# Half the up projections of an attention block, with the swapped rows made by ScalarE, and larger rings of buffers in its experts

## The reference

```python
mod = (_silu(L0_c) @ L0_wmod).reshape(L0_c.shape[0], 6, 1, -1)
sa, ca, ga, sb, cb, gb = (mod[:, 0], mod[:, 1], mod[:, 2], mod[:, 3], mod[:, 4], mod[:, 5])
...
h = _layernorm(x, axis=-1) * (1 + ca) + sa
x = x + ga * _L0_attn_ref(h, ...)
h = _layernorm(x, axis=-1) * (1 + cb) + sb
x = x + gb * _L0_ffn_ref(h, ...)
...
# attention
h = (x - mu) * jax.lax.rsqrt(var + LN_EPS) * ln_scale + ln_bias
c_q = h @ w_down_q.T
c_kv = h @ w_down_kv.T
q = (c_q @ w_up_q.T).reshape(b, s, H, DH).transpose(0, 2, 1, 3)
k = (c_kv @ w_up_k.T).reshape(b, s, H, DH).transpose(0, 2, 1, 3)
v = (c_kv @ w_up_v.T).reshape(b, s, H, DH).transpose(0, 2, 1, 3)
# rotation
rot = jnp.stack([e * cos - o * sin, e * sin + o * cos], axis=-1).reshape(xr.shape)
...
scores = jnp.einsum('bhqd,bhkd->bhqk', q, k) * scale
attn = jax.nn.softmax(scores, axis=-1)
# experts
h = jax.nn.relu(xf * wi @ w1[i] + b1[i])
y = h @ w2[i] + b2[i]
out = jnp.where(wi > 0, y, out)
```

## Time and profile before

| | |
|---|---|
| median of 3 runs | 841.57 us (839.31 to 844.46) |
| profiled execution | 843.6 us, span of its instructions 841.7 us |
| busy: TensorE, VectorE, ScalarE, GpSimd | 806.4, 618.2, 394.2, 652.0 us |
| the same as shares of the span | 96%, 73%, 47%, 77% |
| granted TensorE clock, mean | 0.984 of 2.4 GHz; 0.83 between 790 and 810 us, 1.00 from 60 to 750 us |
| attention | from about 66 to 760 us |
| experts | from there to the end |

### The profile page before, as it was taken

One profiled execution on the slowest core, in us unless ns is written; L12 is line 12 of the kernel. 1 busy time (PEld: TensorE's weight loads), 2 busy tenths in 40 slices (PEclk: granted clock), 3 DMA queues, 4 the chain that ended last, 5 costly groups with the idle time before them and its releaser, 6 DMA issues.

```text
span 841.7 us, 15143 instructions
## 1 busy us (share of the span) xinstructions
PE 806.4 (96%) x5218; PEld 481.3 (57%) x5218; DVE 618.2 (73%) x1204; ACT 394.2 (47%) x636; POOL 652.0 (77%) x341
## 2 busy tenths in 40 slices
PE   4878999999999999999999999999999999999986
PEld 2535556555555555555555555555565555448886
DVE  8887777787778787878777877778777756346644
ACT  3655444444444444444444445544444444435543
POOL 3479998999999797979797989888888787041654
PEclk8979999999999999999999999999999999999989
DMA  9600010101001010101010101010101010452763
GB/s 246 144 1 14 14 27 14 28 14 25 15 13 28 2 39 2 38 3 39 1 39 2 39 1 40 1 27 15 28 1 27 1 27 1 127 181 80 243 217 97
DMA packets 83257, 40.00 MB, mean 48 GB/s; under 512 B 57433, under 2 KB 71136, under 8 KB 83120
## 3 DMA queue, kind: packets, MB, share of 16 engines
q1 hardware_dynamic: 81456, 35.86, 17.9%
q0 software_dynamic: 1728, 3.19, 1.0%
HBM read 31.46 MB, written 8.21 MB: 47 GB/s over the span
## 4 chain that ended last, share of the span: by engine, by line
PE 93%; DVE 3%; DMA 1%; issue 1%; POOL 1%; ACT 0%; POOLq 0%; SPq 0%; DVEq 0%
PE ps_o L488 28%; PE ps_m L451 9%; PE ps_x L439 9%; PE ps_s L472 7%; PE ps_s L474 7%; PE ps_s L478 7%; PE ps_s L476 7%; PE ps_s L539 4%; PE ps_s L677 3%; PE ps_s L497 2%; DVE mx L1219 1%; PE ps_m L506 1%; PE ps_s L687 1%; PE ps_x L687 1%; PE ps_o L687 1%
## 5 line engine op out<-in xcount | busy, mean ns | idle before, releaser
L1040 POOL TENSOR_TENSOR big<-big,probs 128x1024 f32<-128x1024 f32 x180 | 440.3, 2446 | 70.0 <-ACT probs L784 49.9
L1219 DVE TENSOR_REDUCE mx<-ps_m 128x2 f32<-128x1024 f32 x240 | 294.0, 1225 | 108.5 <-PE ps_m L451 108.2
L784 ACT ACTIVATE probs<-ps_s 128x1024 f32<-128x1024 f32 x256 | 248.9, 1024 | 169.1 <-PE ps_s L478 169.0
L488 PE MATMUL ps_o<-probs,c_all 128*64 128x512 f32 x1024 | 247.9, 605 | 0.0
L488 PEld LDWEIGHTS ps_o<-probs,c_all 128*64 128x64 f32 x1024 | 62.1, 136 | 97.2 <-ACT probs L784 41.4
L451 PE MATMUL ps_m<-k_hi,q_hi 64*128 64x512 f32 x480 | 108.4, 444 | 2.2 <-DVE mx L1219 2.2
L472 PE MATMUL ps_s<-q_hi,k_hi 64*128 64x512 f32 x512 | 101.8, 393 | 0.0
L478 PE MATMUL ps_s<-neg_row,one_row 64*128 64x512 f32 x512 | 101.4, 388 | 0.0
L474 PE MATMUL ps_s<-q_hi,k_lo 64*128 64x512 f32 x512 | 101.2, 390 | 0.0
L476 PE MATMUL ps_s<-q_lo,k_hi 64*128 64x512 f32 x512 | 101.2, 389 | 0.0
L451 PEld LDWEIGHTS ps_m<-k_hi,q_hi 64*128 64x128 f32 x480 | 46.6, 183 | 87.3 <-issue 77.0
(11 more groups left out here) (310 smaller groups left out, 997.3 us busy)
## 6 DMA issues: line engine op xcount, KB each, us to landing
big<-in_experts SPq DMA_DIRECT2D x30, 322.0 KB, 3.6
big<-rd_dram SPq DMA_DIRECT2D x60, 128.0 KB, 2.9
big<-in_wqk SPq DMA_DIRECT2D x16, 256.0 KB, 2.7
neg_row<-nm SPq DMA_DIRECT2D x256, 0.5 KB, 2.0
xs_row<-xs_dram SPq DMA_DIRECT2D x6, 390.0 KB, 4.2
big<-in_expert_w SPq DMA_DIRECT2D x8, 256.0 KB, 4.0
xs_dram<-zero SPq DMA_DIRECT2D x2, 990.0 KB, 10.4
xs_dram<-zero SPq DMA_DIRECT2D x2, 960.0 KB, 11.7
```

Source lines behind the costliest of these rows:

```text
L488: ins = nc.tensor.matmul(ps_o[64 * h:64 * h + 64, :], c_all[:, (p // HP) * TB + kt, :], probs[:, st % 4, h, :], start=(kt == 0), stop=(kt ...
L784: nc.scalar.activation(probs[:, st % 4, :, :], ps_s[:, 2 * (st % 2):2 * (st % 2) + 2, :], ACT.Exp, scale=SCALE).then_inc(s["probs"], 1)
L1040: V.tensor_tensor(acc[:, buf(p, half), :, :], first, probs[:, st % 4, :, :], ALU.add).then_inc(s["added"], 1)
L1219: V.reduce_max(mx[:, :, kh, qt], max_banks(q, n), AX.X).then_inc(s["max_reduced"], 1)
```

## The change

In pairs 2 to 15 the twin is left out: a unit is 512 columns of q or k, straight only, two products, made in groups 1, 3, 5 and 7. ScalarE makes the exchanged rows: it copies four blocks of 32 rows from `ps_x` to the SBUF buffer `tmp`, each to the place of its neighbour, after the group's exponentials. VectorE's `turn` is divided into `turn_cos`, `turn_sin` and `turn_sum` and done in the following even group around the second `reduce_max`; `turn_sin` now has both operands and its result in SBUF. ScalarE's `upper` and VectorE's `lower` follow in the next odd group. GpSimd's split has half the columns from pair 2 on. In the experts ScalarE copies the slots of both batches; output buffers are 16 and places for expert weights 10 (the added ones lie in `probs`, free after the attention); SP loads a group's slots ahead of its expert weights, but for batch 1's first group, where the weights come first and the first tile of slots is loaded by itself.

```diff
-NY = 8
+NY = 16
+NI = 10
...
         def unit_banks(q, u):
-            return U_BANKS[u] if q < 2 else (ps_x[:, 0:QUART], ps_x[:, QUART:HALF])
+            return U_BANKS[u] if q < 2 else (ps_x[:], tmp)
...
-                for twin, bank in enumerate(unit_banks(q, u)):
+                for twin, bank in enumerate(unit_banks(q, u)[0:2 if q < 2 else 1]):
...
-                    if p + 2 <= LAST:
-                        up(p + 2, g)
+                    if p + 2 <= LAST and g % 2:
+                        up(p + 2, g // 2)
...
+            def swap(q, u):
+
+                act.wait_ge(s["up_product"], n_up(q, u))
+                act.wait_ge(s["rotated"], n_unit(q, u) - 1)
+                for j in range(4):
+                    ins = nc.scalar.copy(tmp[quarter(j), :], ps_x[quarter(j ^ 1), :])
+                ins.then_inc(s["swapped"], 1)
...
-                    if g == 0 and 2 <= p + 1 <= LAST:
-                        upper(p + 1, NGRP - 1)
-                    if g > 0 and p + 2 <= LAST:
-                        upper(p + 2, g - 1)
+                    if g == 1 and 2 <= p + 1 <= LAST:
+                        upper(p + 1, 3)
+                    if g in (3, 5, 7) and p + 2 <= LAST:
+                        upper(p + 2, g // 2 - 1)
                     expo(p, 2 * g)
                     expo(p, 2 * g + 1)
+                    if g % 2 and p + 2 <= LAST:
+                        swap(p + 2, g // 2)
...
+                if q >= 2:
+                    hi, lo, whole = wh[:, q % 2, :, 0, :], wl[:, q % 2, :, 0, :], wu[:, :, 0, :]
...
+            def turn_cos(q, u):
+
+                straight, swapped = unit_banks(q, u)
+                dve.wait_ge(s["swapped"], n_swap(q, u))
+                V.tensor_tensor(straight, straight, cos_sb[:, unit_columns(q, u)[1]], ALU.mult).then_inc(s["turned"], 1)
+
+            def turn_sin(q, u):
+
+                straight, swapped = unit_banks(q, u)
+                V.tensor_tensor(swapped, swapped, sin_sb[:, unit_columns(q, u)[1]], ALU.mult).then_inc(s["turned"], 1)
+
+            def turn_sum(q, u):
+
+                straight, swapped = unit_banks(q, u)
+                n = n_unit(q, u)
+                dve.wait_ge(s["turned"], 2 * n)
+                V.tensor_tensor(straight, straight, swapped, ALU.add).then_inc(s["rotated"], 1)
...
-                    q, u = (p + 2, g - 1) if g else (p + 1, NGRP - 1)
+                    q, u = (p + 2, g // 2 - 1) if g > 1 else (p + 1, 3)
                     if 2 <= q <= LAST:
-                        lower(q, u)
+                        if g % 2:
+                            lower(q, u)
+                        else:
+                            turn_cos(q, u)
+                            turn_sin(q, u)
                     if p < LAST:
                         reduce_max(p + 1, 2 * g + 1)
                         if g % 4 == 3:
                             neg_max(p + 1, g // 4)
-                    if p + 2 <= LAST:
-                        turn(p + 2, g)
+                    if 2 <= q <= LAST and g % 2 == 0:
+                        turn_sum(q, u)
...
             for k in range(NA * GS, NG * GS):
-                hidden(k % (2 * GS), k)
+                slots_out(k % NI, k)
+                if k > NA * GS:
+                    hidden((k - 1) % NI, k - 1)
+            hidden((NG * GS - 1) % NI, NG * GS - 1)
...
-            def expert_data(g, par, i):
-
-                k = g * GS + i
-                ge(sp, s["y_copied"], k - 2 * GS + 1)
+            def expert_data(k):
+
+                if 6 <= k < NI:
+                    sp.wait_ge(s["out_product"], n_part(LAST, 1))
+                ge(sp, s["y_copied"], k - NI + 1)
...
+                if g == NA:
+                    sp.dma_start(xs[g % NR][:, 0:1, :], rows[:, 0:1, :]).then_inc(tile_in, 16)
+                    sp.dma_start(xs[g % NR][:, 1:GS, :], rows[:, 1:GS, :]).then_inc(group_in[g % NR], 16)
+                else:
+                    sp.dma_start(xs[g % NR], rows).then_inc(group_in[g % NR], 16)
...
-                group(g, g % 2)
+                if g != NA:
+                    slots_in(g)
+                for k in range(GS * g, GS * g + GS):
+                    expert_data(k)
+                if g == NA:
+                    slots_in(g)
```

More of the change, by code:

```diff
@@ L144, in build @@
         h2, xw = hn, h0
[L146 to L149, removed]
+        ring = [big[:, F * E + n * WROW:F * E + (n + 1) * WROW] for n in range(6)]
+        ring += [p_flat[:, n * WROW:(n + 1) * WROW] for n in range(NI - 6)]
+        w1_sb = [r[:, 0:F] for r in ring]
+        b1_sb = [r[:, F:F + F // P] for r in ring]
+        b2_sb = [r[:, F + F // P:WROW] for r in ring]
+        ys = [c_all[:].rearrange("p t d -> p (t d)")[:, n * D:(n + 1) * D] for n in range(8)]
+        ys += [p_flat[:, (NI - 6) * WROW + n * D:(NI - 6) * WROW + (n + 1) * D] for n in range(NY - 8)]
         xT = [moe[:, n, :] for n in range(2)]
@@ L216, in build @@
             "turned": "a product with cos or sin (vector)",
+            "swapped": "its halves of 32 rows changed places, in SBUF (scalar)",
             "rotated": "their sum: a part of the rotated q or k, in PSUM (vector)",
@@ L255, in build @@
             "slots_T": "a tile of slots transposed (tensor)",
-            "slots_in": "and in SBUF (scalar, then vector)",
+            "slots_in": "and in SBUF (scalar)",
             "hidden_product": "a tile's hidden layer (tensor)",
@@ L276, in build @@
         weights_in = sem("weights_in")
-        expert_in = [sem(f"expert_in{n}") for n in range(2 * GS)]
+        expert_in = [sem(f"expert_in{n}") for n in range(NI)]
+        tile_in = sem("tile_in")
         placed = [sem(f"placed{n}") for n in range(NY)]
@@ L310, in n_unit @@
         def n_unit(q, u):
-            return 4 * (q == 1) + u + 1 if q < 2 else 8 * (q - 1) - 4 + u + 1
+            return 4 * (q == 1) + u + 1 if q < 2 else 4 * (q - 1) + u + 1
         def n_up(q, u):
@@ L325, in all_units, with n_swap @@
         def all_units(q):
-            return n_unit(q, 3 if q < 2 else 7)
+            return n_unit(q, 3)
+        def n_swap(q, u):
+            return 4 * (q - 2) + u + 1
         def unit_columns(q, u):
[L330 to L334, removed]
-        def units_of_max(q, n):
[L338 to L343, removed]
+            w, half = UNITS[u]
+            return w, slice(half * HALF, (half + 1) * HALF)
+        def units_of_max(q, n):
+            qt, kh = max_tile(n)
+            return n_unit(q, max(UNITS.index((0, qt // 4)), UNITS.index((1, kh))))
         def max_tile(n):
@@ L880, in _ @@
                         h2_rows(range(2 * g - 6, 2 * g - 4))
-                    if p == LAST - 1 and g in (1, 2):
-                        h2T_out(0, g - 1)
+                    if p == LAST - 1 and g in (2, 3):
+                        h2T_out(0, g - 2)
                     if p == LAST and g == 0:
@@ L908, in _ @@
                 if k + 1 < NA * GS:
-                    slots_out((k + 1) % (2 * GS), k + 1)
-                hidden(k % (2 * GS), k)
+                    slots_out((k + 1) % NI, k + 1)
+                hidden(k % NI, k)
                 if 0 < k <= T_DVE:
-                    y_out((k - 1) % (2 * GS), k - 1)
+                    y_out((k - 1) % NI, k - 1)
                 if k in T_FEAT:
@@ L947, in split @@
                 if q >= 2:
-                    pool.wait_ge(s["up_product"], n_up(q - 2, 3 if q < 4 else 7))
+                    pool.wait_ge(s["up_product"], n_up(q - 2, 3))
                 tiles = lambda a: a.rearrange("p w a c -> p (w a) c")
                 hi, lo, whole = tiles(wh[:, q % 2, :, :, :]), tiles(wl[:, q % 2, :, :, :]), tiles(wu[:])
-                one = ones_sq[:].unsqueeze(1).to_broadcast([P, 4, P])
+                if q >= 2:
+                    hi, lo, whole = wh[:, q % 2, :, 0, :], wl[:, q % 2, :, 0, :], wu[:, :, 0, :]
+                one = ones_sq[:].unsqueeze(1).to_broadcast([P, 4 if q < 2 else 2, P])
                 V.tensor_tensor(hi, whole, one, ALU.mult).then_inc(s["weights_split"], 1)
@@ L1512, in _ @@
                 if k > NA * GS:
[L1513 to L1514 removed]
+                    y_out((k - 1) % NI, k - 1)
+            y_out((NG * GS - 1) % NI, NG * GS - 1)
         @block.sync
```

52 lines of the change are left out of this document (19 added, 33 removed).

## The result

The changed kernel took 819.2 us (median of 4 runs, 819.13 to 819.31), the kernel before beside it 843.02 (4 runs, 839.31 to 845.12): a ratio of 0.973, 95% interval [0.971, 0.975]. I had predicted 821, within 799 to 838, and faster with a chance of 0.85. The profiled execution took 819.3, with a span of 817.5 against 841.7.

What follows compares the result with a forecast made beforehand. TensorE, 93% of the chain of waits, was taken as the bound. Attention's 14.2 us plus the experts' 6.5 gave 20.7 saved: profiled 843.6 to 822.9, or 821 from the median of 841.57, range 799 to 838.

Steps and rivals of the forecast that it cites:

- TensorE's part: Attention, up projections halved: even groups fall to 4.36 us, odd ones keep 5.05; 2.8 us saved per pair.
- ScalarE's exchange: Four copies in odd groups, 2.4 us behind the second exponential, with 0.7 us of cover; cost nothing.
- VectorE's turn: Even groups: cos, sin and second maximum just fit before 4.36; lower bits cost 0.15 us each in groups 5, 7.
- The point that decides: VectorE's sin and divide, with two SBUF inputs, wait for GpSimd's additions; divide stalls group 4 by 0.75 us.
- Pairs with more work for GpSimd: GpSimd's extra steps limit savings to 0.2 us in pairs 1 to 4 and 0.8 in 0 and 10 to 12.
- my second rival: Sin misses the gap between GpSimd's additions in group 2: 2.1 to 2.5 us per pair, 846 in all; chance 0.10.
- Pair 14: Late attention pair with no up projection to make; predicted saving 0.
- The experts: Batch 1's first product 3.9 us sooner, 2.6 more from full pace; together 6.5 us, bounds 3 and 8.
- My third rival: Attention as forecast, but experts give only 1 to 3 us, as GpSimd's scatter sets batch 1's start: 825; chance 0.12.
- The sum: Attention's 14.2 us plus 6.5 after it give 20.7 saved: profiled 843.6 to 822.9, or 821 from the median 841.57.

## Why the prediction was right, point by point

**TensorE's part** (2.8 us a pair): right. Plain even groups took 4.37 and odd ones 5.05, and without two-input instructions a pair took 40.95, where the sum gives 40.7.

**ScalarE's exchange** (cost nothing, cover 0.7): right; 0.73 in the trace, and 1.05 by the doubled exchange, by which an exponential may come 0.3 late unpunished.

**VectorE's turn** (it just fits; 0.15 each in groups 5 and 7): it fits, and the two groups grew by 0.07 each, half of what I had.

**The point that decides**, the two SBUF inputs: right, in mechanism and size. Of the 1.1 us that I added to a pair, 0.75 were the port, by divide into group 4, and 0.3 the lower bits. The port measured 0.64 (41.59 less 40.95), all of it in group 4, with no stall in the groups 0, 2 and 6; what is left over the sum is 0.2. Divide and sin ended 0.55 after an addition's end at each meeting shown. The Trainium skill ("SBUF — State Buffer", "SBUF: two separate sides") says that a VectorE instruction with two SBUF inputs and a GpSimd one that reads SBUF exclude each other for their whole length. By the 0.55 the trace agrees with it.

**Pairs with more work for GpSimd**: this step failed, by its size and its mechanism. I had counted 2.5 us a pair in which GpSimd is held, from the addition of 2.95 in the earlier trace rows, on top of additions whose spacing in the kernel before already had some of it. The additions' mean went from 2.446 before to 2.466, and is 2.382 with no such instruction left: about 0.1 each, 1.2 a pair, and only 0.3 more than before. In pair 6 the 14 additions take 35.8 with their gaps (36.0 forecast) and the split 1.9 (1.29 forecast): 37.7 of GpSimd's time and not 39.8. So GpSimd had room for one more step (pairs 10 to 12 saved 1.9 and not 0.8, 3.3 us more in all), and pairs 1 to 4 saved 2.3 in all and not 0.8. What I took for a queue that fills up is a question of place: an extra step shifts the additions, and a product with sin then misses the gap in group 2. Pair 1 shows that at its worst (6.42 for group 2), and saved nothing; without two-input instructions it took 40.93, with the same steps on GpSimd. That is my second rival's mechanism, in four pairs out of fourteen and but once at its full price.

**Pair 14**: a term that I put at nothing without a reason. The kernel after has the logits in group 4 instead of 3, right ahead of values and outputs, which neither the section on the change nor my sum mentions; it cost 2.2 in the profiled execution, 0.5 by the order and the rest by the clock.

**The experts** (6.5, bounds 3 to 8): 5.1 by the trace, 6.3 by the ratios. The first product of batch 1 came at 779.70 and, measured from the last attention group, 3.7 sooner than before (predicted 3.9); it and the next ran at full pace (6.05 us from the first product to the third before, 3.93 now: 2.1 more against 2.6); 0.7 was lost again in the tiles after them. My third rival, the scatter, did not decide on the first chip; on three others the two waits stand beside it and the experts gain next to nothing, but no run shows the one as the cause of the other.

**The sum**: 20.7 against 24.2 in the profiled executions, and 22.4 from the median that I started from (841.57 to 819.2). Pairs 0 to 13 gave 20.3 without the first group, where I had 14.2; start and first group together gave 0.9; pair 14 took 2.2 and the experts fell 1.4 short. So 821 came within 2 us because errors of 7 too little and 3.6 too much went against each other, which is luck, not because each term was that good.

## What to carry to other kernels

Before an edit puts two SBUF operands into a VectorE instruction, list GpSimd's instructions at that place: the wait is not a tax on all of them but a gap that is hit or missed, and the step that decides is where the queues put it. Often the algebra allows one operand to stay in PSUM (here by multiplying before the rows are exchanged), and single steps of GpSimd can be spread so that none shares a pair with another. When small steps are moved along with a large edit, cost each as an edit of its own.

## What was not expected of the hardware

On three chips, TensorE, ScalarE and VectorE stood still together inside batch 0 of the experts, for 12 us on TensorE, from the time on at which GpSimd had its eight row DMAs under way. The weights concerned had been asked for 20 us and more before, ScalarE copied a tile 9 us after its transpose, and the DMA engines had little to do in the second half. The kernel before is 11 to 13 us slower on these chips. What holds the engines there was not found. And 16 products of 8 columns (1.95 us) ahead of full ones were followed by 5 us at a granted clock of 0.66 in four executions of nine.
